# The last four sequences of a gated cross-attention and expert-attention layer, as one group of four or as two groups of two

## What is computed

```python
def xattn(ctx, latent, Wk, Wq, Wv):           # softmax(q k^T / sqrt(128)) v, one head
    ...
def ffn(x, sim_matrix, gates, q_proj, k_proj, v_proj, o_proj):   # E = 16 experts
    logits = normalise(x) @ normalise(sim_matrix) - sigmoid(gates)
    gated  = relu(logits); mask = ...          # top-2 where no gate is open
    w = softmax(where(mask > 0, gated, -inf))  # one weight per token and expert
    q = einsum('ne,neh->nh', w, einsum('nc,ech->neh', x, q_proj))   # k, v alike
    attn = softmax(q k^T / sqrt(128)) @ v      # within each sequence
    out  = einsum('enh,ehc->nc', einsum('ne,nh->enh', w, attn), o_proj)
x = x + tanh(g_xattn) * xattn(ctx, layernorm(x), ...)
x = x + tanh(g_ffn)   * ffn(layernorm(x), ...)
```

## Time and profile before

| | us |
|---|---|
| median of 3 runs | 885.28 (885.21 to 885.91) |
| profiled execution, its own time | 885.93 |
| its span | 884.1 |
| PE busy | 828.6 (94% of the span) |
| DVE busy | 613.5 |
| POOL busy | 552.1 |
| ACT busy | 519.3 |
| DMA traffic | 150.49 MB, 170 GB/s |

### The profile page before, as it was taken

How to read it: one execution, slowest core, us unless ns; L and a number is a source line. 1 busy time by engine, 2 the same in 40 slices (tenths; PEclk the granted TensorE clock), 3 DMA queues, 4 the chain that set the end, 5 groups by cost and what they waited for, 6 DMA issues and landing times.

```text
span 884.1 us, 16223 instructions
## 1 busy us (share of the span) xinstructions
PE 828.6 (94%) x4344; PEld 458.8 (52%) x4344; DVE 613.5 (69%) x1575; ACT 519.3 (59%) x1148; POOL 552.1 (62%) x588
## 2 busy tenths in 40 slices
PE   4579999999999999999999999999999999999976
PEld 3445555555555555555555555555555555545432
DVE  3777567777685867768676786867677676766545
ACT  3555657565665756566575656656575565656353
POOL 2264567575675757567575756657575765857464
PEclk9999999999999999999999999999999999999988
DMA  8753554453645555364654536464463636466342
GB/s 224 188 191 107 188 196 156 165 183 127 225 128 198 191 174 176 115 217 144 198 176 175 198 104 221 133 203 166 175 202 121 228 103 216 151 205 214 97 154 72
DMA packets 58531, 150.49 MB, mean 170 GB/s; under 512 B 5568, under 2 KB 22144, under 8 KB 58496
## 3 DMA queue, kind: packets, MB, share of 16 engines
q1 hardware_dynamic: 57776, 150.00, 50.3%
q10 hardware_dynamic: 720, 0.08, 0.1%
HBM read 145.34 MB, written 4.72 MB: 170 GB/s over the span
## 4 chain that ended last, share of the span: by engine, by line
PE 33%; issue 29%; POOL 28%; DVE 5%; ACT 3%; POOLq 1%; DMA 1%; ACTq 0%; DVEq 0%
POOL stage L457 13%; POOL zq L452 9%; PE acc_q L890 7%; PE acc_k L890 7%; PE acc_v L890 7%; PE acc_o L906 6%; POOL rstd L437 2%; POOL norm L446 1%; POOL rstd L425 1%; DVE zo_full L753 1%; DVE zq_full L743 1%; PE oT_p L982 1%; PE m L928 1%; PE m L1029 1%; DMA sim_sb<-in_L_ffn_sim_matrix_dram 1%
## 5 line engine op out<-in xcount | busy, mean ns | idle before, releaser
L452 POOL TENSOR_TENSOR zq<-zq_full,zq 128x512 f16<-128x512 f32 x192 | 224.8, 1172 | 218.6 <-ACT zq L505 218.6
L505 ACT ACTIVATE zq<-zq_full 128x512 f16<-128x512 f32 x256 | 161.0, 629 | 201.0 <-DVE zq_full L743 195.6
L457 POOL TENSOR_TENSOR stage<-zo_full,stage 128x512 f16<-128x512 f32 x208 | 240.7, 1160 | 58.2 <-ACT stage L513 58.2
L906 PE MATMUL acc_o<-stage,w_hi 128*128 128x512 f16 x512 | 195.8, 388 | 7.7 <-POOL stage L457 4.2
L743 DVE TENSOR_TENSOR zq_full<-wq_bc,x2T_p 128x512 f32<-128x512 f32 x256 | 173.2, 678 | 34.5 <-ACT x2T_p L606 29.8
L890 PE MATMUL acc_q<-zq,w_hi 128*128 128x512 f16 x512 | 194.5, 380 | 0.0
L890 PE MATMUL acc_k<-zq,w_hi 128*128 128x512 f16 x512 | 194.5, 380 | 0.0
L890 PE MATMUL acc_v<-zq,w_hi 128*128 128x512 f16 x512 | 194.3, 380 | 0.0
L753 DVE TENSOR_TENSOR zo_full<-stage,oT_p 128x512 f32<-128x512 f32 x256 | 172.5, 679 | 7.0 <-PE oT_p L982 6.4
L513 ACT ACTIVATE stage<-zo_full 128x512 f16<-128x512 f32 x256 | 160.0, 628 | 25.1 <-DVE zo_full L753 25.1
L906 PE MATMUL acc_o<-stage,w_lo 128*128 128x512 f16 x256 | 99.1, 387 | 0.0
(11 more groups left out here) (141 smaller groups left out, 1057.4 us busy)
## 6 DMA issues: line engine op xcount, KB each, us to landing
wq_bc<-w_rows SPq DMA_DIRECT2D x128, 512.0 KB, 4.8
stage<-w_rows SPq DMA_DIRECT2D x128, 512.0 KB, 3.7
out_dram<-x_all SPq DMA_DIRECT2D x16, 256.0 KB, 4.3
ctx_g<-in_ctx_dram SPq DMA_DIRECT2D x16, 154.0 KB
x_all<-in_x_dram SPq DMA_DIRECT2D x2, 256.0 KB, 6.8
x_all<-in_x_dram SPq DMA_DIRECT2D x1, 512.0 KB, 9.2
w_rows<-wT SPq DMA_DIRECT2D x16, 32.0 KB, 3.2
wq_sb<-in_L_xattn_Wq_dram SPq DMA_DIRECT2D x1, 64.0 KB, 5.6
```

What stands on the lines that cost most here:

```text
L452: nc.gpsimd.tensor_tensor(zq[:, 1, e % Z_SLOTS, :], zq_full[:, e % F_SLOTS, :], zq[:, 0, e % Z_SLOTS, :], ALU.subtract).then_inc(zq_lo_poo ...
L457: nc.gpsimd.tensor_tensor(zo[:, 1, e % Z_SLOTS, :], zo_full[:, e % F_SLOTS, :], zo[:, 0, e % Z_SLOTS, :], ALU.subtract).then_inc(zo_lo_poo ...
L505: nc.scalar.activation(zq[:, 0, e % Z_SLOTS, :], zq_full[:, e % F_SLOTS, :], ACT.Copy).then_inc(zq_hi_done, 1)
L906: last = nc.tensor.matmul(acc[O][:], w[:, O, e, :], zo[:, half, e % Z_SLOTS, :], start=(e == 0 and n == 0), stop=(e == E - 1 and n == 2))
```

## The change

The number of groups becomes 17. Groups 0 to 14 keep four sequences, groups 15 and 16 have two. Every instruction on the tokens of a small group takes its first 256 columns, or two of four sequences (cols, size, begin). What keeps its full size for them: the gate's operations, which work on tiles of four sequences by 16 experts, the write and the spread transfers of the weights, and wT. The loop ends two bodies earlier relative to NG, at 12 instead of 13; bodies 12 to 18 are written out. The core of the diff, with the same replacement in all other places that take a group's columns:

```diff
-    NG = B // G
+
+    HALF = G // 2
+    NG = B // G + 1
     N = G * P
-    LOOP = (3, NG - 3)
+    LOOP = (3, NG - 5)
...
+        def small(g):
+            return isinstance(g, int) and g >= NG - 2
+
+        def size(g):
+            return HALF if small(g) else G
+
+        def begin(g):
+            return B - HALF * (NG - g) if small(g) else G * g
+
+        def cols(g):
+            return slice(0, size(g) * P)
...
-                nc.vector.tensor_tensor(zq_full[:, e % F_SLOTS, :], wq_bc[:, e // 2 % W_SLOTS, e % 2], x2T_p[:],
+                nc.vector.tensor_tensor(zq_full[:, e % F_SLOTS, cols(g)], wq_bc[:, e // 2 % W_SLOTS, e % 2, cols(g)],
+                                        x2T_p[:, cols(g)],
                                         ALU.mult).then_inc(zq_full_done, 1)
...
-                        last = nc.tensor.matmul(acc[m][:], w[:, m, s, :], zq[:, half, s % Z_SLOTS, :],
+                        last = nc.tensor.matmul(acc[m][:, cols(i)], w[:, m, s, :], zq[:, half, s % Z_SLOTS, cols(i)],
                                                 start=(s == 0 and n == 0), stop=(s == E - 1 and n == 2))
...
-                    last = nc.tensor.matmul(acc[O][:], w[:, O, e, :], zo[:, half, e % Z_SLOTS, :],
+                    last = nc.tensor.matmul(acc[O][:, cols(g)], w[:, O, e, :], zo[:, half, e % Z_SLOTS, cols(g)],
                                             start=(e == 0 and n == 0), stop=(e == E - 1 and n == 2))
...
-                    if b == G - 1:
+                    if b == size(g2) - 1:
                         last.then_inc(logit_ps, 1)
```

107 lines of the change are left out of this document (56 added, 51 removed).

## The result

The changed kernel takes **889.32 us** (median of 8 runs, 886.97 to 890.18) beside 885.76 for the kernel before (8 runs, 885.21 to 886.06): ratio 1.0038, 95% interval 1.0027 to 1.0048. It is slower by 3.6 us; the forecast was 1.3 less, and the time lies 0.3 above the end of its range. The profiled execution took 890.18, its span is 888.4, that is 4.3 more than the span of before. On another chip the same kernel came out at 887.81 us, ratio 1.0017 (1.0007 to 1.0027), inside the range. Its lines stand 13 to 20 lower than in the kernel before (L743 is now L759, L753 L770, L890 L910, L951 L971, L982 L1002).

The account below looks back on a forecast made before the run. PE matmul work was taken to bound the kernel until 839.8 us, then a 44.3 us tail of engines waiting in turn. The terms, -1.8 + 11.8 + 7.2 - 19.5 + 1.0 = -1.3, took 885.28 to 884.0 us; range 879.5 to 889.0.

Parts of the forecast that it names:

- Body 14, +0.45: Body 14: small g1 adds 1.95, halved g2 saves 0.5, earlier logits take 1.0 off the oT_p wait; net +0.45 us.
- The plan's first step: Reading of the load before the change: up to 840 us PE busy without a gap, DVE and POOL about 61%.
- weight loads don't set the pace, and that rival: Rival: weight loads pace the small matmuls, 0.13 a pair instead of 0.109, 4.0 us slower, 888.0; chance 6%.
- Matmul work, +11.8: Bodies 15 and 16: 55.7 us of matmul work against 43.9, so 11.8 us more before the last v matmul.
- Waits, +7.2: PE waits in bodies 15 and 16: 1.7 at logits, 3.2 before oT_p, 2.3 at body 16's start; 7.2 us more.
- S: Start of body 15's expert steps: 795.94 us before the change, forecast at 794.2 after it.
- the rival of late transfers: Rival: short bodies delay spread transfers, 7.94 us from write to product becoming 9.7; 885.8 us; chance 4%.
- The rival that the waits are hidden: Rival: body 15's waits are absorbed; half of the 7.2 us gives 880.4, all of them 876.8; chance 30%.
- Clock, +1.0: One low clock stretch of 3.4 us at the wait before oT_p, costing 1.0 us on the way to wT.
- My rival of a clock that falls more than once: Rival: two more low clock stretches in bodies 15 and 16, each costing 1.7 us; 887.4 us; chance 18%.
- Tail, -19.5: After the last v matmul: half-width work shortens the tail from 44.3 to 24.8 us, 19.5 less.
- POOL did halve (0.63 a product), so that rival: Rival: POOL's products stay at 1.11, about nine on the tail's chain costing 0.49 more each; 888.4 us; chance 4%.

Follow-up runs that it names:

- e17: Changed kernel, with POOL holding its two remainders of round 5 in bodies 14 and 15 until DVE has made the gate's mask: 889.2 us, ratio 1.0038.
- e18: e8 with POOL's two remainders of round 5 held until DVE has made the gate's mask, in all expert bodies with a gate: 879.43 us, ratio 0.9926.
- e8: Changed kernel with half-size spreads and two-sequence gates for small groups, q, k, v of group 15 copied earlier, last spread ahead of the store: 885.04 us.
- e14: Changed kernel itself, unchanged, one more single profiled execution: 889.23 us.
- e1: Changed kernel with the two small groups' spread transfers cut to the 256 columns used, 256 KB instead of 512 KB: 885.62 us, ratio 0.9991.
- e4: Changed kernel with zero-weight matmuls, which add nothing to the result, filling PE's three waits in body 15: 886.93 us, ratio 1.0003.
- e2: Changed kernel with the gate operations of the two small groups on two sequences instead of four: 886.41 us, ratio 1.0004.

## Why the prediction was wrong

The plan of the sum held and its large terms were met within 2.4 us each; but they cancel to 1.3, and three of the misses, body 14, the clock and the tail, make the kernel slower. The waits came out shorter than forecast, by less.

- **Bodies 12 and 13:** right (50.83 and 48.86 us).
- **Body 14, +0.45: failed, +1.39.** The step that failed is "that takes 1.0 of the wait of 1.10 us ahead of oT_p away". Of that wait 0.20 went, from 1.10 to 0.90. DVE did start the gate 1.2 us earlier (10.87 us after v's transposes for 12.06), but from there to oT_p it took 10.93 us for 10.08, since its second comparison then ran beside a POOL remainder (1.19 for 0.21). I had taken 10.08 us from one place in time to another as if it belonged to DVE alone. e17 gives back 0.40 of it, and in e18, which differs from e8 by the hold alone, the wait is gone. The plan's first step read the load too low as well: the 61% for DVE and POOL are those of 794 to 840; from 741 to 791, where body 14 lies, they are 73% and 65%.
- **Matmul work, +11.8:** right in kind, +12.6 in size. Small matmuls stand 0.11 apart, so weight loads don't set the pace, and that rival falls.
- **Waits, +7.2:** right in place, 1.97, 1.25 and 2.41 for 1.7, 3.2 and 2.3, in all 5.95. The one before oT_p is shorter because PE comes late through the low clock. oT_p itself came at S + 20.6 for a forecast of 20.2. Where the clock stays up at the start of body 16 (e14), S to the last v matmul is 63.6, for a forecast of 62.9 + 1.0. The way from the write of the weights to the first product took 8.07 for 7.94 (827.65 less 819.58), so the rival of late transfers falls for body 15; DVE stands 4.80 before that product, for a forecast of 4 to 5. The rival that the waits are hidden, my second likeliest case, falls with them.
- **Clock, +1.0: mis-sized, +3.3 of matmul time.** Of it 1.1 only takes the place of a wait (before oT_p, 1.25 for e1's 2.31). I expected one low stretch, behind the longest wait. There are two in four of five executions, behind the waits of 1.97 and 2.41; the first falls in front of a wait and is nearly free (oT_p stands 18.96 us after v's transposes, 18.70 in e4 with a full clock), the second costs 1.9 to 2.4. My rival of a clock that falls more than once had its place and about its price right, and too small a chance. Its threshold, a wait between 1.1 and 3.1 us, does not exist in that form: 2.41 left the clock alone in one execution and not in four others. The trace of before spoke against it already, in a place that I did not read. In its tail the clock falls once more, with no single wait of PE above 1.57 us since 859:

```profile
868.29 0.39 PE L906 MATMUL acc_o<-stage,w_hi 128*128 128x512 f16 x1 [1.57 <-POOL stage L457]
```

```profile
870.00:876.00 6.00, 5.12 (x14) 1.60 (x13) 3.66 (x6) 3.68 (x6) 4.77 (x5) 0.50 0.00 0
```

- **Tail, -19.5: mis-sized, -17.1.** Last v matmul to oT_p took 7.0 for 6.5; outT's copy came 16.4 us after oT_p, for 0.8 + 13.3 = 14.1. One sentence that failed is "it still lands ahead of POOL": the last transfer starts where I put it, but DVE can use it only 5.2 us later (876.53 to 881.74) and not 4.0, and waits 1.32 and 0.89 for the last two pairs. The other is that no term has a clock for the tail. At a full clock and with transfers of full size (e2) the tail is 26.1, and with smaller transfers as well (e8) 25.3, close to the 24.8 of the forecast. By these single profiles some 1.1 us of the miss are clock, 0.8 transfers, and the rest stays open. POOL did halve (0.63 a product), so that rival falls.

In the table's terms: -1.3 + 0.9 (body 14) + 0.4 (start) + 1.8 (bodies 15 and 16, clock above all) + 2.4 (tail) = +4.2, for 4.3 measured. The single causes are shown by the runs, each size by one or a few profiles, apart from the start's 0.4, which varies between executions of the same kernel, and the clock's fall, whose own cause stays open. The place of the time at the very end of the range is in part chance: one low stretch of the clock more or less is worth 2 us, and the same kernel was outside the range in one set of runs (889.32) and inside it in the other (887.81). Open is, too, why the two chips give 1.0038 and 1.0017.

## What to carry to other kernels

A smaller last group shortens the tail, but its two halves pay for it with fixed costs: chains between engines and transfers that don't shrink, beside work that does. When two large terms cancel, put the range by what can break, and ask which way each breaks: here the clock, late transfers and two engines in each other's way could only add time to a sum that had little or nothing for them. And an interval measured on one engine may be moved in time only if what it contends with moves along.
